# Context stage of a token mixer and expert kernel: four row buffers, earlier statistics, two banks for the first products, scatter one step earlier, first token loads of the next stage behind their own rows

## The chip, the core and the metric

The kernel runs on one core of a Trainium2 chip. TensorE (PE in the profile) multiplies, VectorE (DVE), ScalarE (ACT) and GpSimd (POOL) work on elements, SyncE (SP) only issues transfers; GpSimd issues the indirect ones. They run side by side and wait for one another on semaphores. The metric is the device time of one execution, in microseconds (us).

## What is computed

2048 tokens of width 512 go through two blocks. The first, which the change touches, is this (cut from the reference):

```python
x = x + _L0_xattn_ref(_layernorm(x), token_ids, ctx, ctx, ctx)

def _L0_xattn_ref(hidden_states, token_ids, Wg, Wu, Wd):      # Wg = Wu = Wd = ctx, 4 matrices of 512 x 512
    expert_ids = jnp.minimum(jnp.clip(token_ids, 0, 24999) // 6250, 3)
    for e in range(4):
        g = jax.nn.silu(jnp.einsum('bsd,fd->bsf', hidden_states, Wg[e]))
        u = jnp.einsum('bsd,fd->bsf', hidden_states, Wu[e])
        y = jnp.einsum('bsf,df->bsd', g * u, Wd[e])
        out = jnp.where((expert_ids == e)[..., None], y, out)
```

The second block normalizes x again, adds a shared gated product and the four best of 32 experts for every token, and a residual.

## The kernel before, in words

**Stages.** `context` is the first block of instructions, `shared_routing_and_experts` the second. All five engines meet at a barrier between the two; none starts the second before each has come to the end of its list in the first.

**The context stage.** First the tokens are sorted by group: counts and ranks by small products on TensorE and some thirty small operations on VectorE, which end in a list of row numbers (`gather1`, `scatter1`; semaphore `listed` at 1) and a table with the group of every tile and the number of tile pairs (`listed` at 2). A tile is 128 tokens of one group. The inputs make 18 tiles, n = 0 to 17. Matrices are split into a high and a low half, so that a product is three matmuls: 12 for one 128x512 result over 512 inputs (lines 222 to 224). `high(e)` on ScalarE and `low(e)` on VectorE (line 550) split the four context matrices; `low(2)` and `low(3)` run inside the first steps.

For each tile: gather of 128 rows of x by GpSimd (L381); `stats1`, mean and variance, on VectorE (L630, L633); `rstd1`, inverse root, scale and bias, three instructions on GpSimd (L386 to L391); `keep`, a copy of the rows for the residual, and `h`, the normalized rows, on ScalarE (L512, L529); `t1`, four transposes ("the turn") on TensorE (L447), whose result ScalarE and VectorE split into halves (`t1hi`, `t1lo`); `g1`, 12 matmuls into `ps_z`; `silu` on ScalarE and `a`, its product with `ps_z`, on VectorE (L645); `t2`, the turn of a, with `t2hi` and `t2lo`; `g2`, 12 matmuls into `ps_y`; `x1`, the sum with the kept rows and its statistics, on VectorE (L659 to L665); `rstd2` on GpSimd (L398 to L405); `x2` and `base` on ScalarE (L534, L539), `hn` on VectorE (L671); `scatter`, the indirect write of 128 rows to `hb_dram` by GpSimd (L413), which takes its row numbers from a copy made by `rows` (L642).

**What sets the order.** `pipeline` (in the listing) writes each engine's list. In step k an engine does each of its parts, in the order of its list, for tile k minus the part's skew. The first 12 steps are written out, the others up to step 17 run in a loop, then the rest is written out. TensorE has `[("t1", 3), ("t2", 5), ("g1", 4), ("g2", 6)]`, ScalarE `[("base", 9), ("x2", 8), ("t1hi", 3), ("t2hi", 5), ("keep", 2), ("weights", 0), ("h", 2), ("silu", 4)]`. `weights` splits a piece of the shared weights in steps 6, 7 and 8 (ScalarE L507).

**Buffers.** Gathered rows have two buffers, so gather n waits until `keep` and `h` of tile n - 2 are done. There is one bank `ps_z` for the first products. `hb`, what is scattered, has two buffers, and `base`, `rows` and `hn` of tile n wait until scatter n - 2 has landed. A `keep_busy` of 24 small matmuls, which are not used, stands ahead of the turns of tiles 0 and 1 and at the end of the stage.

**The end of the stage.** GpSimd waits until every scatter has landed and raises `stored`. On this TensorE starts its last `keep_busy` and SyncE loads the first four tiles of the next stage, tokens 0 to 511, from `hb_dram` (L339). The next stage turns its 16 tiles, by token number, in pairs with the routing logits of the pair before; tiles 4 to 15 are loaded by SyncE (L781) when a turn has freed the buffer.

## Time and profile before

| | us |
|---|---|
| median of 3 runs (lowest to highest) | 703.03 (700.66 to 703.36) |
| profiled execution, its own time | 702.91 |
| its span, first to last instruction | 701.2 |
| TensorE busy, matmuls | 628.1 (90%) |
| VectorE busy | 439.6 (63%) |
| ScalarE busy | 368.2 (53%) |
| GpSimd busy | 333.8 (48%) |
| mean granted TensorE clock, share of full | 0.975 |

The page of the profile cuts the span in 40 equal slices of 17.5 us. The context stage fills the first nine and a half of them. In its line of the granted clock all slices show 9 tenths or more but the tenth one, which shows 6, and the last. TensorE's busy time counts overlapping matmuls once and is no measure of how well it is used. The chain of waits follows the execution back from its last instruction; where it names an engine, that engine's work ended last there.

### The profile page before, as it was taken

The page shows a single profiled execution, that of the slowest core. Times are in us where ns is not written, and L with a number is a line of the kernel's source. Part 1 is how long each engine was busy: PE and PEld are TensorE (multiplying, and loading weights), DVE is VectorE, ACT ScalarE, POOL GpSimd, SP SyncE. Part 2 cuts the span into 40 slices and gives each one's busy share as a digit, 9 for nine tenths or more (in the row PEclk, how much of TensorE's full clock was granted, in tenths as well). Part 3 has the DMA queues.
Part 4 walks back from the last instruction along what each step waited for, and adds up shares of the span by engine and source line. Part 5 has one row for each costly group of instructions (what it writes and reads, how often), then busy time and mean ns, then how long its engine had stood idle before and what let it go on. Part 6 is the DMA issues. An engine that isn't in the chain of part 4 may idle for free.

```text
span 701.2 us, 15255 instructions
## 1 busy us (share of the span) xinstructions
PE 628.1 (90%) x3239; PEld 510.7 (73%) x3241; DVE 439.6 (63%) x1019; ACT 368.2 (53%) x637; POOL 333.8 (48%) x373
## 2 busy tenths in 40 slices
PE   2489999962999999799999999999999999999990
PEld 2368888852877887588878788788787688788870
DVE  7558787661799998365565565675465565655620
ACT  4357766533533322356665655765565565656530
POOL 2537777652002111545646456546546546465632
PEclk9999999996999999999999999999999999999995
DMA  6511332324793653667799788997777997988645
GB/s 243 181 46 41 118 106 90 116 110 141 241 344 49 147 136 46 137 180 208 203 240 266 207 266 205 278 279 202 211 205 184 277 269 195 269 218 219 108 62 70
DMA packets 35790, 124.69 MB, mean 178 GB/s; under 512 B 4784, under 2 KB 5936, under 8 KB 31152
## 3 DMA queue, kind: packets, MB, share of 16 engines
q0 software_dynamic: 24256, 59.26, 38.8%
q1 hardware_dynamic: 11504, 65.09, 26.4%
q8 instruction: 12, 0.20, 0.1%
q14 instruction: 18, 0.15, 0.1%
HBM read 90.51 MB, written 39.06 MB: 185 GB/s over the span
## 4 chain that ended last, share of the span: by engine, by line
PE 50%; DMA 20%; issue 10%; DVE 8%; POOL 6%; POOLq 2%; ACT 2%; DVEq 1%; ACTq 0%; SPq 0%
PE sps_gu L222 8%; PE sps_gu L224 7%; PE sps_gu L223 7%; DMA out<-r_oh,e_sidx 6%; DMA out<-r_rank,e_sidx 5%; DMA out<-normw,e_sidx 4%; PE sps_t L222 3%; PE sps_t L224 3%; PE sps_t L223 3%; PE sps_rank L866 2%; PE ps_z L222 2%; PE ps_z L224 2%; PE ps_z L223 2%; DMA raw<-in_experts_w 1%; PE sps_table L866 1%
## 5 line engine op out<-in xcount | busy, mean ns | idle before, releaser
L1275 DVE TENSOR_TENSOR wl<-raw,wh x87 | 105.7, 1225 | 58.6 <-ACT wh L1062 54.2
L222 PE MATMUL sps_gu<-wh,s_xth 128*128 x320 | 132.4, 414 | 2.5 <-DVE s_xtl L1258 2.1
L224 PE MATMUL sps_gu<-wh,s_xtl 128*128 x320 | 126.1, 394 | 0.0
L223 PE MATMUL sps_gu<-wl,s_xth 128*128 x320 | 125.0, 391 | 0.0
L854 POOL DMA_INDIRECT out<-r_oh,e_sidx x40 | 68.0, 1701 | 97.3 <-issue 64.1
L1062 ACT ACTIVATE wh<-raw x87 | 91.1, 1060 | 18.2 <-DMA raw<-in_experts_w 9.4
L840 POOL DMA_INDIRECT both<-hb_dram,e_gidx x76 | 84.1, 1106 | 31.7 <-issue 17.4
L222 PEld LDWEIGHTS sps_gu<-wh,s_xth 128*128 128x128 f32 x320 | 60.2, 188 | 14.5 <-issue 4.5
L1037 ACT ACTIVATE both<-sps_gu 128x256 f32<-128x256 f32 x80 | 30.7, 384 | 76.0 <-PE sps_gu L224 76.0
L222 PE MATMUL sps_t<-wh,s_ath 128*128 x160 | 69.6, 435 | 0.5
L224 PEld LDWEIGHTS sps_gu<-wh,s_xtl 128*128 128x128 f32 x320 | 60.1, 188 | 13.7
L223 PEld LDWEIGHTS sps_gu<-wl,s_xth 128*128 128x128 f32 x320 | 60.4, 189 | 10.5
L818 POOL DMA_DIRECT2D out<-both x16 | 14.1, 884 | 103.1 <-ACT both L1025 52.9
L224 PE MATMUL sps_t<-wh,s_atl 128*128 x160 | 63.1, 394 | 0.0
L223 PE MATMUL sps_t<-wl,s_ath 128*128 x160 | 62.7, 392 | 0.0
L1255 DVE TENSOR_TENSOR both<-both,sps_gu 128x256 f32<-128x256 f32 x80 | 33.3, 416 | 44.4 <-ACT both L1037 43.9
L1258 DVE TENSOR_TENSOR s_xtl<-sps_rank,s_xth 128x512 fp32r<-128x512 f32 x40 | 27.4, 686 | 37.9 <-ACT s_xth L1041 37.9
L854 POOL DMA_INDIRECT out<-normw,e_sidx x20 | 34.9, 1744 | 31.8 <-DMA out<-r_oh,e_sidx 28.1
L1049 ACT ACTIVATE r_oh<-sps_t,weight 128x512 f32<-128x512 f32 x40 | 27.4, 686 | 29.1 <-PE sps_t L224 19.6
L854 POOL DMA_INDIRECT out<-r_rank,e_sidx x20 | 31.6, 1581 | 22.8 <-DVE e_gidx L1248 9.5
L224 PEld LDWEIGHTS sps_t<-wh,s_atl 128*128 128x128 f32 x160 | 30.0, 188 | 6.8
L1258 DVE TENSOR_TENSOR s_xtl<-sps_cols,s_xth 128x512 fp32r<-128x512 f32 x40 | 27.5, 688 | 11.8 <-ACT s_xth L1041 11.6
(305 smaller groups left out, 1428.1 us busy)
## 6 DMA issues: line engine op xcount, KB each, us to landing
raw<-in_experts_w SPq DMA_DIRECT2D x32, 1536.0 KB, 8.1
craw<-in_ctx_w SPq DMA_DIRECT2D x4, 1024.0 KB, 8.2
both<-hb_dram SPq DMA_DIRECT2D x16, 256.0 KB, 3.6
out<-hb_dram SPq DMA_DIRECT2D x4, 1024.0 KB, 17.8
out<-both POOLq DMA_DIRECT2D x16, 256.0 KB, 4.2
both<-hb_dram,e_gidx POOLq DMA_INDIRECT x76, 5.8
out<-r_oh,e_sidx POOLq DMA_INDIRECT x40, 5.4
sraw<-in_sg SPq DMA_DIRECT2D x1, 512.0 KB, 5.4
```

The lines of the kernel that those rows point to most:

```text
L222: pe.matmul(acc, left_hi, right_hi, start=start, stop=False)
L223: pe.matmul(acc, left_hi, right_lo, start=False, stop=False)
L224: return pe.matmul(acc, left_lo, right_hi, start=False, stop=stop)
L840: pool.indirect_dma_start(e_xg[:, t.ring], None, hn_rows, bass.IndirectOffsetOnAxis(ap=gidx[:, t.ring:t.ring + 1], axis=0)).then_inc(e_gx[ ...
L854: pool.indirect_dma_start(m.out, bass.IndirectOffsetOnAxis(ap=sidx[:, t.ring:t.ring + 1], axis=0), e_y[t.ring], None, compute_op=ALU.add). ...
L866: mm = pe.transpose(dst[:, c * P:(c + 1) * P], src[:, c * P:(c + 1) * P], m.ident[:])
L1037: nc.scalar.activation(a[:, t.par], ps_gu[t.par][:, 0:INNER], ACT.Silu).then_inc(e["sil"], 1)
L1049: nc.scalar.activation(e_y[t.ring], e_py[t.par][:], ACT.Copy, scale=m.weight2[:, bass.ds(t.n, 1)]).then_inc(e["y"], 1)
L1062: nc.scalar.activation(m.wh[:, bass.ds(x % W_SETS, 1), ROWS[part], :], m.raw[:, bass.ds(x % 2, 1), ROWS[part], :], ACT.Copy).then_inc(e["h ...
L1255: dve.tensor_tensor(a[:, t.par], a[:, t.par], ps_gu[t.par][:, INNER:D], ALU.mult).then_inc(e["a"], 1)
L1258: dve.tensor_tensor(e_xtl[:, t.par].rearrange("p c n -> p (c n)"), e_t1[t.par][:], e_xth[:, t.par].rearrange("p c n -> p (c n)").bitcast(F ...
L1275: dve.tensor_tensor(m.wl[:, w, ROWS[part], :], m.raw[:, bass.ds(x % 2, 1), ROWS[part], :], m.wh[:, w, ROWS[part], :].bitcast(F32), ALU.sub ...
```

## The change

It touches the context stage and the first waits of SyncE in the next one.

- Gathered rows have four buffers for tiles 0 to 3 (`slot`, `landed`); from tile 4 on the first two alternate as before. `hb` moves into the space of the last raw context matrix (`craw`), `x2` gets a place of its own.
- GpSimd gathers tile 0, then 1 and 2 together, then 3 behind the first inverse root (`in_front`). VectorE does the statistics of tile 2 right behind those of tile 1. ScalarE does h of tile 1 right behind h of tile 0, ahead of the high half of tile 0.
- `ps_z` has two banks; `g1` of a tile no longer waits for `a` of the tile before, and TensorE's order is t1, g1, t2, g2.
- VectorE's order is `rows`, `hn`, `stats1`, ..., and `third` (which holds `low(2)`) stands behind the low halves. `scatter` has skew 9 instead of 10 and stands between `rstd1` and `rstd2`.
- A small reduction (`spread`) over the ranks, a product on TensorE and three operations on VectorE give the number of the last tile that holds a token of the first 512. SyncE's first four loads wait for as many scatters, and for statistics, kept copy and h of all tiles, and no longer for `stored`. The wait for all scatters stands in the next stage, ahead of the load of tile 4.
- TensorE's last `keep_busy` waits for the last x2.

The diff, cut to its core; the renamed semaphores and tensors are left out:

```diff
+        craw = sb("craw", [P, E1, C, D])
+        xg = m.tokens
...
-        x2 = m.tokens[:, 2:4]
-        hb = sb("c_hb", [P, 2, 2, D])
+        x2 = sb("c_x2", [P, 2, D])
+        hb = craw[:, E1 - 1].rearrange("p c n -> p (c n)").rearrange("p (s a n) -> p s a n", s=2, a=2)
...
-        ps_t1, ps_t2, ps_z = (ps(n, [P, D]) for n in ("ps_t1", "ps_t2", "ps_z"))
+        sidx = m.sidx1
+        ps_t1, ps_t2 = (ps(n, [P, D]) for n in ("ps_t1", "ps_t2"))
+        ps_z = [ps(f"ps_z{i}", [P, D]) for i in range(2)]
...
+        def slot(t):
+
+            return t.n if isinstance(t.n, int) and t.n < RING else t.par
+
+        def landed(eng, t):
+
+            eng.wait_ge(gx[slot(t)], 16 if isinstance(t.n, int) and t.n < RING else 16 * t.half)
+
+        def in_front(n):
+
+            if not isinstance(n, int) or n > RING - 1:
+                return ()
+            return {0: (0,), 1: (1, 2), 2: (3,), 3: ()}[n]
...
-            for q in gx:
+            for q in gx[0:2]:
...
-            sp.wait_ge(m.s["stored"], 1)
+            sp.wait_ge(m.s["early"], 1)
+            tiles = number_of_pairs(sp, m.tab1[0:1, 1, 0:1], MAX1) * 2
+            reach_of_first = sp.value_load(m.tab1[0:1, 1, 1:2], min_val=2, max_val=MAX1)
+            sp.wait_ge(s["stat1"], tiles)
+            sp.wait_ge(s["xr"], tiles)
+            sp.wait_ge(s["h"], tiles)
+            m.carry(sp)
+            sp.wait_ge(hbs[0], 16 * ((reach_of_first + 1) // 2))
+            sp.wait_ge(hbs[1], 16 * (reach_of_first // 2))
             for i in range(RING):
                 sp.dma_start(m.tokens[:, i], m.hb_dram[i * P:(i + 1) * P, 0:D]).then_inc(m.s[f"rows{i}"], 16)
...
-                if part == "gather":
-                    wait(pool, s["xr"], t.n - 1)
-                    wait(pool, s["h"], t.n - 1)
-                    wait(pool, gx[t.par], 16 * t.half)
+                if part == "gather" and isinstance(t.n, int) and t.n < RING:
+                    pool.wait_ge(m.s["listed"], 1)
+                    for n in in_front(t.n):
+                        pool.indirect_dma_start(xg[:, n], None, m.x, bass.IndirectOffsetOnAxis(ap=m.gather1[:, n:n + 1], axis=0)
+                                                ).then_inc(gx[n], 16)
+                elif part == "gather":
+                    left = t.n - RING if isinstance(t.n, int) and t.n < RING + 2 else t.n - 2
+                    pool.wait_ge(s["xr"], left + 1)
+                    pool.wait_ge(s["h"], left + 1)
+                    pool.wait_ge(gx[t.par], 16 * (t.half - 1))
                     if moving(t.n):
                         pool.wait_ge(s["gi"], t.n - STATIC + 1)
                         rows = gidx[:, t.par:t.par + 1]
                     else:
-                        wait(pool, m.s["listed"], 1)
                         rows = m.gather1[:, t.n:t.n + 1]
                     m.carry(pool)
...
-            pipeline(pool, pairs, [("scatter", 10), ("rstd1", 2), ("rstd2", 7), ("gather", 0)], emit)
-            m.carry(pool)
-            count = number_of_pairs(pool, m.tab1[0:1, 1, 0:1], MAX1)
-            for q in hbs:
-                pool.wait_ge(q, 16 * count)
-            pool.sem_inc(m.s["stored"], 1)
+            pipeline(pool, pairs, [("rstd1", 2), ("scatter", 9), ("rstd2", 7), ("gather", 0)], emit)
...
+            pe.wait_ge(m.s["spread"], 1)
+            pe.matmul(ps_spread, spread[:, 0:1], m.ident[:], start=True, stop=True).then_inc(m.s["spread_row"], 1)
...
-                        keep_busy(pe, m, ps_z, WARM)
+                        keep_busy(pe, m, ps_z[1], WARM)
...
-                    wait(pe, s["a"], t.n)
-                    product(ps_z, hth, htl, t).then_inc(s["g1"], 1)
+                    wait(pe, s["a"], t.n - 1)
+                    product(ps_z[t.par], hth, htl, t).then_inc(s["g1"], 1)
...
-            pipeline(pe, pairs, [("t1", 3), ("t2", 5), ("g1", 4), ("g2", 6)], emit,
+            pipeline(pe, pairs, [("t1", 3), ("g1", 4), ("t2", 5), ("g2", 6)], emit,
...
-            pe.wait_ge(m.s["stored"], 1)
-            keep_busy(pe, m, ps_z, WARM)
+            pe.wait_ge(s["x2"], 2 * number_of_pairs(pe, m.tab1[0:1, 1, 0:1], MAX1))
+            keep_busy(pe, m, ps_z[0], WARM)
...
-                    act.wait_ge(gx[t.par], 16 * (t.half + 1))
+                    if isinstance(t.n, int) and 1 <= t.n < LED:
+                        return
+                    landed(act, t)
...
+                elif part == "h" and isinstance(t.n, int) and t.n < LED:
+                    for n in range(LED) if t.n == 0 else ():
+                        if n >= 1:
+                            act.wait_ge(gx[n], 16)
+                            nc.scalar.activation(xr[:, n], xg[:, n], ACT.Copy).then_inc(s["xr"], 1)
+                        act.wait_ge(s["bias1"], n + 1)
+                        act.wait_ge(gx[n], 16)
+                        nc.scalar.activation(h[:, n], xg[:, n], ACT.Identity, bias=rs1[:, n, 2:3], scale=rs1[:, n, 1:2]).then_inc(s["h"], 1)
...
+            dve.tensor_reduce(spread[:, 0:1], sel[:, 1, 0:RING], AX.X, ALU.max).then_inc(m.s["spread"], 1)
...
+            dve.wait_ge(m.s["spread_row"], 1)
+            k(dve.tensor_reduce(spread[0:1, 1:2], ps_spread, AX.X, ALU.max))
+            k(dve.tensor_scalar(spread[0:1, 2:3], spread[0:1, 1:2], 1.0, 2.0, ALU.add, ALU.max))
+            dve.tensor_copy(m.tab1[:, 1, 1:2], spread[0:1, 2:3]).then_inc(m.s["early"], 1)
...
+                    if isinstance(t.n, int) and t.n < RING:
+                        for n in in_front(t.n):
+                            dve.wait_ge(gx[n], 16)
+                            wait(dve, s["bias1"], n - 1)
+                            dve.bn_stats(stat[:, 0, n % 2, :], xg[:, n]).then_inc(s["stat1"], 1)
+                            dve.wait_ge(s["stat1"], n + 1)
+                            dve.bn_aggr(mv[:, 0, n % 2, :], stat[:, 0, n % 2, :]).then_inc(s["mv1"], 1)
+                        return
+                    landed(dve, t)
...
-            pipeline(dve, pairs, [("stats1", 2), ("index", 0), ("third", 0), ("x1", 7), ("t1lo", 3), ("t2lo", 5), ("rows", 9), ("hn", 9), ("weights", 0), ("a", 4)], emit)
+            pipeline(dve, pairs, [("rows", 9), ("hn", 9), ("stats1", 2), ("index", 0), ("x1", 7), ("t1lo", 3), ("t2lo", 5), ("third", 0), ("weights", 0), ("a", 4)], emit)
...
+            pairs = number_of_pairs(sp, m.tab1[0:1, 1, 0:1], MAX1)
+            for q in ("stored0", "stored1"):
+                sp.wait_ge(m.s[q], 16 * pairs)
```

On GpSimd, the head of the stage, before and after: L381 and L400 are gathers, L386 to L391 and L418 to L423 the first inverse root of a tile.

```order
L381 DMA both<-in_x,gather 128x512 [waits chain0,listed]
L381 DMA both<-in_x,gather 128x512 [waits listed]
L386 TENSOR_SCALAR c_rs<-c_mv 128x1 [waits c_mv1]
L388 TENSOR_TENSOR c_rs<-c_rs,minus_half 128x1 [waits c_var1]
L391 TENSOR_SCALAR c_rs<-c_mv,c_rs 128x1 [waits c_rstd1]
L381 DMA both<-in_x,gather 128x512 [waits listed,c_gx0,c_xr,c_h]
```

```order
L400 DMA both<-in_x,gather 128x512 [waits chain0,listed]
L400 DMA both<-in_x,gather 128x512 [waits listed]
L400 DMA both<-in_x,gather 128x512
L418 TENSOR_SCALAR c_rs<-c_mv 128x1 [waits c_mv1]
L420 TENSOR_TENSOR c_rs<-c_rs,minus_half 128x1 [waits c_var1]
L423 TENSOR_SCALAR c_rs<-c_mv,c_rs 128x1 [waits c_rstd1]
L400 DMA both<-in_x,gather 128x512 [waits listed]
```

The third gather moved ahead of the first inverse root, and the third and fourth no longer wait for h (`c_h`) or the kept copy (`c_xr`).

On VectorE, the same place: `ctl` is a low half of a context matrix, `c_halves` the low half of a turned tile, `tab` the table whose entry the register load reads.

```order
L550 TENSOR_TENSOR ctl<-craw,cth 128x2048 [waits ctx_hi]
L189 TENSOR_LOAD tab [waits listed]
L189 ISA x2
L630 BN_STATS c_stat<-both 128x6 [waits c_gx0]
L633 BN_AGGR c_mv<-c_stat 128x2 [waits c_stat1]
L630 BN_STATS c_stat<-both 128x6 [waits c_gx1]
L633 BN_AGGR c_mv<-c_stat 128x2 [waits c_stat1]
L550 TENSOR_TENSOR ctl<-craw,cth 128x2048 [waits ctx_hi]
L648 TENSOR_TENSOR c_halves<-ps_t,c_halves 128x512 [waits c_t1hi]
```

```order
L589 TENSOR_TENSOR ctl<-craw,cth 128x2048 [waits ctx_hi]
L654 TENSOR_REDUCE spread<-ps_prefix 1x1 [waits spread_row]
L655 TENSOR_SCALAR spread<-spread 1x1 [waits chain1]
L656 CAST tab<-spread 1x1 [waits chain1]
L190 TENSOR_LOAD tab [waits listed]
L190 ISA x2
L677 BN_STATS c_stat<-both 128x6 [waits c_gx0]
L679 BN_AGGR c_mv<-c_stat 128x2 [waits c_stat1]
L677 BN_STATS c_stat<-both 128x6 [waits c_gx1]
L679 BN_AGGR c_mv<-c_stat 128x2 [waits c_stat1]
L677 BN_STATS c_stat<-both 128x6 [waits c_bias1,c_gx2]
L679 BN_AGGR c_mv<-c_stat 128x2 [waits c_stat1]
```

Three operations stand between `low(1)` and the register load, and the statistics of tile 2 have taken the place of `low(2)`, which now follows the low half of tile 0.

On GpSimd, the end of the stage, before and after: L413 and L445 are scatters, the others the second inverse root of a tile (L398 to L405, L430 to L437).

```order
L404 TENSOR_SCALAR c_affine<-c_rs 128x1 [waits c_rstd2]
L405 TENSOR_SCALAR c_affine<-c_rs,c_mv 128x2
L413 DMA hb_dram<-c_hb,c_sidx 2048x1024 [waits c_base,c_hn,c_hb1,c_si]
L89 ISA
L413 DMA hb_dram<-c_hb,c_sidx 2048x1024 [waits c_base,c_hn,c_hb0,c_si]
L413 DMA hb_dram<-c_hb,c_sidx 2048x1024 [waits c_base,c_hn,c_hb1,c_si]
L189 TENSOR_LOAD tab
L189 ISA x2
L421 ISA
L259 UNCONDITIONAL_BRANCH [waits c_hb0,c_hb1]
```

```order
L445 DMA hb_dram<-craw,sidx 2048x1024 [waits c_base,c_hn,stored1,c_si]
L430 TENSOR_SCALAR c_rs<-c_mv 128x1 [waits c_mv2,c_x2]
L431 TENSOR_SCALAR c_rs<-c_mv 128x1
L433 TENSOR_TENSOR c_rs<-c_rs,minus_half 128x2 [waits c_var2]
L436 TENSOR_SCALAR c_affine<-c_rs 128x1 [waits c_rstd2]
L437 TENSOR_SCALAR c_affine<-c_rs,c_mv 128x2
L89 ISA
L445 DMA hb_dram<-craw,sidx 2048x1024 [waits c_base,c_hn,stored0,c_si]
L445 DMA hb_dram<-craw,sidx 2048x1024 [waits c_base,c_hn,stored1,c_si]
L260 UNCONDITIONAL_BRANCH
```

Three scatters stood behind the inverse root of the last tile, and behind them a wait for all landings; now two stand behind it, one has moved ahead of it, and GpSimd leaves the stage without that wait.

## Rows read from the trace of the kernel before

**Rows 1.** windows: length, busy PE PEld DVE ACT POOL (instructions), granted clock, DMA share, GB/s

```profile
32.00:45.00 13.00, 7.95 (x35) 5.86 (x34) 6.74 (x10) 4.99 (x9) 6.21 (x8) 0.87 0.24 61
...
152.00:172.00 20.00, 2.74 (x24) 2.47 (x24) 4.22 (x10) 3.96 (x5) 7.96 (x14) 0.57 0.35 138
```

**Rows 2.** chain that ended last: start, length, what; turns of two steps

```profile
50.38 0.87 PE ps_t L447 x8
...
56.75 0.87 PE ps_t L447 x8
```

**Rows 3.** timeline of the head: start, length, engine, line [idle before]; last: the chain

```profile
15.72 1.31 DVE L203 SCALAR_TENSOR_TENSOR tb1f<-tb1f 1x11 f32<-1x11 f32 x7
...
17.68 2.27 DVE L550 TENSOR_TENSOR ctl<-craw,cth 128x2048 fp32r<-128x2048 f32 x1
...
19.88 0.68 DVE L630 BATCH_NORM_STATS2 c_stat<-both 128x6 f32<-128x512 f32 x1
...
21.37 2.74 PE L230 MATMUL ps_z<-before_b,ones_b 128*128 128x128 bf16 x24 [7.91 <-DVE c_mv L633]
...
22.61 1.93 POOL L391 TENSOR_SCALAR c_rs<-c_mv,c_rs 128x1 f32<-128x1 f32 x1 [0.21 <-POOL c_rs L388]
...
29.96 0.49 PE L222 MATMUL ps_z<-cth,c_halves 128*128 x1
...
32.45 2.70 POOL L388 TENSOR_TENSOR c_rs<-c_rs,minus_half 128x1 f32<-128x1 f32 x1
...
36.52 0.66 PE L447 MATMUL ps_t<-ident,c_h 128*128 128x128 f32 x4 [3.54 <-ACT c_h L529]
...
39.34 0.43 PE ps_z L224
```

**Rows 4.** register load of the pair count (line 189), by operation

```profile
L189 DVEq TENSOR_LOAD <-tab x1: 553/553/553, 17.8 to 17.8; - x1
```

**Rows 5.** timeline of ACT in a step that also splits shared weights

```profile
57.72 0.59 ACT L524 ACTIVATE c_halves<-ps_t 128x512 fp32r<-128x512 f32 x1
...
58.72 1.06 ACT L507 ACTIVATE wh_s<-sraw 128x1024 fp32r<-128x1024 f32 x1
...
59.66 0.81 ACT L529 ACTIVATE c_h<-both,c_rs 128x512 f32<-128x512 f32 x1
```

**Rows 6.** timeline of POOL and ACT in the steps of the loop

```profile
98.21 1.22 POOL L401 TENSOR_TENSOR c_rs<-c_rs,minus_half 128x2 f32<-128x2 f32 x1
...
102.08 1.02 POOL L413 DMA_INDIRECT hb_dram<-c_hb,c_sidx  x1 [0.30 <-issue]
...
108.80 1.02 POOL L413 DMA_INDIRECT hb_dram<-c_hb,c_sidx  x1 [0.30 <-issue]
...
125.20 0.82 ACT L529 ACTIVATE c_h<-both,c_rs 128x512 f32<-128x512 f32 x1 [2.30 <-POOL c_rs L391]
```

**Rows 7.** end of the stage: chain pieces for the DMAs and x1, timeline for the rest

```profile
150.63 3.42 DMA hb_dram<-c_hb,c_sidx
...
151.25 0.39 PE L224 MATMUL ps_y<-cth,c_halves 128*128 x1
...
155.25 0.70 DVE c_x L659
...
159.81 0.81 ACT L534 ACTIVATE both<-c_x,c_affine,c_rs 128x512 f32<-128x512 f32 x1 [0.96 <-POOL c_affine L405]
...
165.52 3.21 DMA hb_dram<-c_hb,c_sidx
...
168.82 2.74 PE L230 MATMUL ps_z<-before_b,ones_b 128*128 128x128 bf16 x24 [17.18 <-POOLq L422]
...
168.84 1.76 SPq L339 DMA_DIRECT2D both<-hb_dram  x4
```

**Rows 8.** timeline of PE at the start of the next stage

```profile
172.13 1.33 PE L866 MATMUL sps_t<-ident,both 128*128 128x128 f32 x8 [0.57 <-PEq L259]
...
176.89 1.30 PE L866 MATMUL sps_t<-ident,both 128*128 128x128 f32 x8
```

30 lines of the change are left out of this document (15 added, 15 removed).

## Prediction, made before the changed kernel was run

> **What bounds the kernel now.** I read the slices of the page first: TensorE is busy nearly everywhere, and its clock is clearly below full in one slice only, the one in which the context stage ends. So I took windows of that stage [rows 1]. Between 32 and 45 us TensorE works 7.95 of 13 us, and between 152 and 172 us only 2.74 of 20, all of it the dummy products that warm it, at a granted clock of 0.57: mostly the lower, 1.2 GHz, of its two levels. Between the two it never rests: the chain of waits shows one tile a step, every 6.37 us [rows 2]. Of that the two turns take 0.87 and each group of twelve products (6.37 - 0.87) / 2 = 2.75. Nothing in the change touches this work, so the stage can only win at its head, at its end, and lose in the middle. I write E for the end of the last product of the stage, 151.25 + 0.39 = 151.64 us [rows 7].
>
> The head is a line of handovers [rows 3]: `low(1)` on VectorE until 19.95, statistics of tile 0, inverse root on GpSimd (one of its instructions takes 1.93 us beside `low(2)`), h, turn, first product at 29.96. Tile 2 is late because its rows were only asked for when tile 0 was normalized, and then its inverse root takes 2.70 us beside `low(3)`: TensorE waits 3.54 us until 36.52. The turn of tile 4, with which the even steps begin, comes at 50.38 [rows 2].
>
> At the end [rows 7] x1 of the last tile waits for scatter 13 to land (150.63 + 3.42), then GpSimd and ScalarE bring x2 at 159.81, the last scatter goes at 165.52 = E + 13.9 and lands 3.21 later, at E + 17.1. Only then do the warming products and the first token loads start, at 168.8. The next stage turns its first tile at 172.13 = E + 20.5 and its fifth at 176.89 = E + 25.3 [rows 8].
>
> **The head, step by step.** Four gathers without a wait for a free buffer take tiles 2 and 3 off the critical path, and `low(2)` now stands behind the first low half, not beside the first inverse root. Against that, VectorE has four more small operations ahead of the first statistics. Such operations stand 1.31 / 7 = 0.19 us apart [rows 3]: one ahead of `low(0)`, three behind `low(1)`, 0.75 in all. The register load of the pair count, today hidden under `low(1)`, now stands behind them, 0.55 us [rows 4] and some 0.25 for the two register steps behind it. Statistics of tile 0 move from 19.88 to about 21.4. The Trainium skill (DMA: Bandwidth & Descriptors, § Latency and other measured facts) gives about 0.6 us as the floor of such a load, near the trace's 0.55.
>
> From there, with durations of the same rows: mean and variance at 22.5, warming products until 25.3 (2.74), turn of tile 0 at 25.4. ScalarE now does h of tile 1 ahead of the high half of tile 0, so low half 0 is ready at 28.9, the first product starts at 29.4 (29.96 today) and ends at 32.3. The turn of tile 2 needs low half 1, which stands behind `low(2)` and the statistics of tile 3: 32.9. Twelve products follow at 33.4 at once (no a is needed with two banks), until 36.2; `low(3)` runs beside them. The turn of a(0) at 36.2, its high half, the kept copy and h of tile 3 on ScalarE in that order give the turn of tile 3 at 38.9; then 12 + turn + 12 products until 45.2, and behind the first piece of shared weights the turn of tile 4 at **45.7 instead of 50.38: 4.7 won**. The granted clock of 0.87 in this stretch today [rows 1] followed the 3.5 us of waiting; a product stood 0.43 apart then [rows 3] where 2.75 / 12 = 0.23 is the pace at 2.4 GHz. I count on full clock, since the longest gap in my line is 2.2 us. If seven products run at the lower level as now, 7 x 0.20 = 1.4 of the 4.7 are gone. At the other end, with the register load hidden, I would win 5.5.
>
> **The middle.** TensorE now turns a behind the first products instead of ahead of them. Within a step the order is t1, twelve products, t2, twelve products, so the high half of a starts at about +3.9 us, and the kept copy and h stand behind it on ScalarE: 1.0 for the first two, 0.8 for h [rows 5], h ready at +5.7, under the 6.37 of a step by 0.6. In the steps with a piece of shared weights 0.94 more lies between (58.72 to 59.66 [rows 5]), so the next turn is late by 0.35. One such step is in the 45.7 already, two follow: **0.7 lost**. Today h has over 2 us of room there and this cost nothing.
>
> GpSimd is the second thing in the middle. In the loop its scatters stand 6.72 apart [rows 6], more than TensorE's 6.37: it falls behind 0.35 each step, and by 125.20 h waits 2.30 us for it, just about when TensorE begins to lose (some 0.5 us in all before the end). The change keeps its instructions but gives it less room: `rows` and `hn` come first on VectorE and a comes later, so the statistics of a tile are ready some 2.7 us later in the step; in return h may come 0.6 later than today before TensorE waits. GpSimd's 6.7 us are 1.3 for the first inverse root, 1.4 for the scatter, 2.3 for the second root and 1.6 for the gather. The statistics are ready at +2.5 and the gather ahead of them ends at +2.8, so the first root is ready at +4.1; TensorE would wait from +5.5, a lead used up after four steps of the loop; from the fifth on each step costs 0.35, 0.9 in all, against today's 0.5: **0.4 lost**. Bounds: 0 if GpSimd's gaps shrink with the shorter issue, 3.2 if all nine steps with a scatter run at its pace.
>
> At this place one rule speaks against the change. In [rows 6] an instruction at 98.21 takes 1.22 us while VectorE does `hn` beside it. The Trainium skill (GPSIMD Engine Reference, § 8 Key points) says that GpSimd shares its SBUF interfaces with VectorE and contends with instructions of two SBUF inputs, as `hn` is. The trace agrees (2.70 beside `low(3)` too). By it a worse meeting of `hn` and GpSimd could add up to 0.5 us a step, 3 us in six steps of the loop; since `hn` runs once a step before and after, my sum has none.
>
> E then falls at 151.64 - 4.7 + 0.7 + 0.4 = 148.0.
>
> **The end, counted from E.** Scatter 13 goes ahead of the second inverse root instead of behind it and lands well before E, so x1 of tile 17 starts at +0.1, not at 155.25 = +3.6. It gains less than that behind it, because GpSimd has inverse root 16 until +2.0 and scatter 15 (1.1 us) ahead of inverse root 17: that ends at +5.8, x2 at +5.9 to +6.7 (today 159.81 = +8.2). The last scatter, behind hn and base of tile 17, goes at +7.5 instead of +13.9 and lands at **+10.8 instead of +17.1**.
>
> The warming products wait for x2, not for the last landing: +6.7. From their start to the first turn it takes 172.13 - 168.82 = 3.3 [rows 7, 8], so the next stage begins at +10.0 instead of +20.5. Its first four tiles are there: the loads wait for the last h (some 20 us ahead of E) and for the scatters that hold rows 0 to 511. The inputs give 108, 119, 131 and 1690 tokens to the four groups, 18 tiles, and the first 512 tokens end in the eighth, so this wait ends last at h. What is late next are tiles 4 on, since SyncE now waits for all scatters there: issue at +10.9, 3.3 until the first such load landed (168.84 to 172.13): +14.2. Four turns and the first logits end there too (+10.0 plus 4.0), so the fifth turn comes at about +14.5 instead of +25.3: **10.8 won**, or 9.5 if the twelve loads that now go out at once land one by one, 1.3 apart. From there the stage is TensorE's own work as before, and all later stages move with it. The new SyncE waits have nothing queued behind them but these loads.
>
> **Sum.** 4.7 - 0.7 - 0.4 + 10.3 (between 9.5 and 10.8) = 13.9 us. The profiled execution took 702.9 us, the median of the three is 703.0; 702.9 - 13.9 = **689.0**. Bounds of the terms: head 3.3 to 5.5, middle -3.9 to -0.2, end 9 to 11: 8.4 to 16.3 won, or 686.6 to 694.5.
>
> **Rivals.** (a) *GpSimd sets the pace of the whole middle*, from the first scatter, and meets `hn` worse: 3.2 + 3 lost there instead of 0.4, and the head's clock falls: 689.0 + 5.8 + 1.4 = 696.2. For it speaks the 6.72 us; against it that GpSimd had over 2 us in hand until 125 us. (b) *The early loads do not help*: the next stage waits for transfers in any case, as its first turns do today. Then the fifth turn comes as far behind the last landing as today, 25.3 - 17.1 = 8.2, at 10.8 + 8.2 = +19, and 4.5 of the gain are lost: 693.5. Against it speaks that SyncE's queue is empty from 24 us on. (c) *Slower*: the clock. The new order puts short gaps into every step (h ready only 0.6 ahead), where today there are none from 45 to 150 us, with full clock. If such gaps bring the clock down, a product costs 0.43 instead of 0.23 us, 24 of them 4.8 us a step: three such steps eat the 13.9, and five make 689.0 + 24 = 713. Both low stretches of this stage followed a gap of over 3 us, so I give it little. The Trainium skill has such a case (TensorE: Matmul & The Clock Gate, § A second HAM failure mode: psum-queue depth-cycling): a kernel that went round its PSUM banks and paused briefly between groups swung between the two clock levels. No row here shows it. (d) *More*: the register load is hidden, GpSimd keeps up, and routing starts ahead of a busy stretch of DMA: 685.
>
> **How the numbers follow.** The forecast's case 0.62, (a) with its milder forms 0.14, (b) 0.08, (c) 0.04, (d) 0.07, and 0.05 that gains and losses cancel within 3.5 us. About 0.5% (3.5 us) is what a measurement of this kernel can tell from no change. Faster by more than that: 0.62 + 0.14 + 0.08 + 0.07 = 0.91, less 0.03 for later stages that I did not follow: 0.88; same 0.05 + 0.02 = 0.07; slower 0.04 + 0.01 = 0.05. The range 685 to 697 leaves out (c), the cancelling case and the ends of (a) and (d).
>
> **What would show it.** The turn of tile 4 at 45 to 46 us (above 48: the head is wrong); no clock below 1 between 30 and 45; steps of 6.4 us with one or two of 6.7 to 6.8 where shared weights are split, and again in the last two or three steps of h; E near 148; x2 of the last tile 6 to 7 us behind E, the last scatter 7 to 8 behind; SyncE's four loads issued near 125 to 130; the first turn of the next stage 10 us behind E and the fifth near 14.5. Steps of 6.7 all along would be (a), a late fifth turn (b), a granted clock below 1 in the middle (c).

## The result and the profile after

The changed kernel takes **696.72 us** (median of 4 runs, 695.64 to 696.88) where the kernel before took 702.58 beside it: ratio 0.9926, 95% interval 0.9906 to 0.9947. Run again beside the experiments it was 697.26 against 701.71, 0.9941 (0.9911 to 0.9970). So it is faster by 4 to 6 us. I had forecast 689.0, 13.9 less: the sign and the range hold, the size is more than twice what came. The profiled execution after took 696.7 us, its span 694.8 us (before: 701.2). Three executions beside the experiments, of 712 to 1286 us, were in a slower state and are left out of the ratios.

These instants divide the difference. In this table and below, E is again the end of the last product of the stage, and "turn n" the turn of tile n. Turns are read from timelines: turn 4 of before is there at 50.22, where the chain of [rows 2] has the same one at 50.38.

| | before | forecast | after |
|---|---|---|---|
| turn of tile 4 of the context stage | 50.2 | 45.7 | 47.3 |
| E | 151.6 | 148.0 | 156.0 |
| last scatter issued | E + 13.9 | E + 7.5 | E + 8.3 |
| first turn of the next stage | E + 20.5 | E + 10.0 | E + 12.6 |
| fifth turn of the next stage | E + 25.3 = 176.9 | E + 14.5 = 162.5 | E + 18.0 = 174.0 |
| from the fifth turn to the end of the span | 524.3 | as before | 520.8 |

2.9 us were won in the head, **7.2 lost in the middle** (turn 4 to E: 108.6 us, before 101.4), 7.2 won at the end. That makes 2.9 at the fifth turn, not 14.4. Another 3.5 us of the two spans' difference arose in the last 520 us, whose code is unchanged but for SyncE's wait ahead of the load of tile 4.

Windows of the kernel after (length, busy PE, PEld, DVE, ACT, POOL, granted clock, DMA share, GB/s), which answer [rows 1]:

```profile
32.00:45.00 13.00, 10.63 (x48) 8.28 (x46) 7.19 (x11) 4.61 (x9) 5.48 (x8) 0.87 0.15 40
152.00:172.00 20.00, 10.11 (x59) 8.75 (x57) 8.12 (x17) 7.72 (x11) 9.29 (x19) 0.69 0.32 127
```

TensorE works 2.7 us more of the first window, as hoped, and yet its clock is 0.87, as before. The second window now holds real products until 156: the stage has slid into it.

Timeline of TensorE after, at turn 3 and at three turns of the loop (start, length, engine, line, operation [idle before <- what ended it]); compare [rows 3] and [rows 2]:

```profile
39.02 0.66 PE L476 MATMUL ps_t<-ident,c_h 128*128 128x128 f32 x4 [1.91 <-ACT c_h L568]
...
40.26 0.63 PE L223 MATMUL ps_z<-cth,c_halves 128*128 x1
40.69 0.63 PE L224 MATMUL ps_z<-ctl,c_halves 128*128 x1
...
87.26 0.66 PE L476 MATMUL ps_t<-ident,c_h 128*128 128x128 f32 x4 [0.41 <-ACT c_h L568]
...
94.50 0.65 PE L476 MATMUL ps_t<-ident,c_h 128*128 128x128 f32 x4 [0.63 <-ACT c_h L568]
...
101.80 0.66 PE L476 MATMUL ps_t<-ident,c_h 128*128 128x128 f32 x4 [0.54 <-ACT c_h L568]
```

After a gap of 1.91 us the products stand 0.43 us apart: that is the lower of the clock's two levels. In the loop a step takes 7.24 and 7.30 us instead of 6.37, and each turn waits for h. Why h is late shows GpSimd in the same stretch, which answers [rows 6]:

```profile
94.31 1.08 POOL L445 DMA_INDIRECT hb_dram<-craw,sidx  x1 [0.79 <-issue]
95.47 0.18 POOL L430 TENSOR_SCALAR c_rs<-c_mv 128x1 f32<-128x1 f32 x1
...
95.99 1.16 POOL L433 TENSOR_TENSOR c_rs<-c_rs,minus_half 128x2 f32<-128x2 f32 x1
...
98.34 1.09 POOL L413 DMA_INDIRECT both<-in_x,c_gidx  x1 [0.51 <-issue]
99.50 0.18 POOL L418 TENSOR_SCALAR c_rs<-c_mv 128x1 f32<-128x1 f32 x1
...
101.65 1.08 POOL L445 DMA_INDIRECT hb_dram<-craw,sidx  x1 [0.83 <-issue]
```

Here GpSimd waits for nothing that the profile shows ("issue"; I read it as the register work ahead of an indirect DMA, which the profile doesn't show by itself): it is never free, and its scatters (L445) stand 7.34 us apart. The idle time ahead of a scatter is 0.79 and 0.83, where [rows 6] had 0.30. The steps of TensorE were 6.4 us from turn 6 to turn 9, at 80.25, and 7.0 to 7.4 from there to turn 16; the loop starts at turn 9 (step 12). For ScalarE it reads like this, x2 waiting for the second inverse root and h for the first (waits between 60 and 150 us: total, times, longest):

```profile
ACT c_x L573 <- POOL c_affine L437: 22.7, 12, 2.4
...
ACT c_h L568 <- POOL c_rs L423: 5.2, 8, 0.7
```

The end of the stage, answering [rows 7 and 8]: GpSimd's last scatter, the end of each engine's list (L260, by operation: count, duration in ns, start), and TensorE's next turns.

```profile
164.21 0.97 POOL L445 DMA_INDIRECT hb_dram<-craw,sidx  x1 [0.88 <-DVE craw L723]
```

```profile
L260 ACTq DRAIN  x1: 1119/1119/1119, 162.1 to 162.1; - x1
L260 DVEq DRAIN  x1: 730/730/730, 162.6 to 162.6; - x1
L260 PEldq DRAIN  x1: 2125/2125/2125, 163.2 to 163.2; - x1
L260 POOLq DRAIN  x1: 4324/4324/4324, 164.0 to 164.0; - x1
```

```profile
162.58 2.74 PE L231 MATMUL ps_z<-before_b,ones_b 128*128 128x128 bf16 x24 [6.62 <-ACT c_x L573]
168.59 1.94 PE L921 MATMUL sps_t<-ident,both 128*128 128x128 f32 x8 [3.27 <-PEq L260]
```

TensorE was done at 165.3, but the barrier opened at 168.5 only: GpSimd's drain takes from 164.0 to 168.3. SyncE's four early loads had gone out at 137.9, so they were there; the next ones went out at 169.77, behind the barrier and the first turn.

The 3.27 us of idle time ahead of the first turn cost more than themselves. Windows of TensorE, before first, then after (length, busy, granted clock, DMA share, GB/s):

```profile
172.00:176.00 4.00, 3.14 (x21) 1.00 0.76 231
```

```profile
168.00:172.00 4.00, 3.41 (x17) 0.50 0.23 80
```

Before, the first turns ran at full clock; now they run at the lower level, and from the first to the fifth turn it takes 5.4 us instead of 4.8.

### The profile page after: what moved, and what is told of

It is laid out like the page before. It is cut to its first block, busy times and chain, and to the rows that moved or that the text cites. A ratio compares the mean times of both kernels' runs of the same rounds, so it can differ in the third digit from the quotient of the medians.

```text
span 694.8 us, 15275 instructions
## 1 busy us (share of the span) xinstructions
PE 632.7 (91%) x3242; PEld 512.0 (74%) x3243; DVE 442.1 (64%) x1023; ACT 366.8 (53%) x637; POOL 334.1 (48%) x373
## 4 chain that ended last, share of the span: by engine, by line
PE 41%; DMA 14%; issue 8%; DVE 4%; POOLq 2%; ACT 2%; POOL 1%; DVEq 1%; ACTq 1%
PE sps_gu L223 8%; PE sps_gu L225 8%; PE sps_gu L224 8%; DMA out<-r_oh,e_sidx 5%; DMA out<-normw,e_sidx 4%; PE sps_t L223 3%; PE sps_t L225 3%; PE sps_t L224 3%; DMA out<-r_rank,e_sidx 2%; PE sps_rank L921 2%; PE sps_table L921 1%; DMA both<-hb_dram,e_gidx 1%; PE sps_cols L921 1%; PE sps_table L976 1%; ACT wh L1117 1%
## 5 line engine op out<-in xcount | busy, mean ns | idle before, releaser
L895 POOL DMA_INDIRECT both<-hb_dram,e_gidx x76 | 82.4, 1085 | 31.4 <-issue 17.4
L225 PEld LDWEIGHTS sps_gu<-wh,s_xtl 128*128 128x128 f32 x320 | 60.0, 188 | 13.9
L873 POOL DMA_DIRECT2D out<-both x16 | 14.2, 885 | 101.2 <-ACT both L1080 58.0
L1310 DVE TENSOR_TENSOR both<-both,sps_gu 128x256 f32<-128x256 f32 x80 | 33.4, 417 | 44.6 <-ACT both L1092 40.8
L909 POOL DMA_INDIRECT out<-r_rank,e_sidx x20 | 31.7, 1585 | 25.4 <-DMA out<-normw,e_sidx 13.5
L1104 ACT ACTIVATE r_oh<-sps_t,weight 128x512 f32<-128x512 f32 x40 | 27.4, 686 | 29.8 <-PE sps_t L225 18.4
## 6 DMA issues: line engine op xcount, KB each, us to landing
out<-hb_dram SPq DMA_DIRECT2D x4, 1024.0 KB, 17.4
```

What stands on the lines that cost most here:

```text
L225: return pe.matmul(acc, left_lo, right_hi, start=False, stop=stop)
L895: pool.indirect_dma_start(e_xg[:, t.ring], None, hn_rows, bass.IndirectOffsetOnAxis(ap=gidx[:, t.ring:t.ring + 1], axis=0)).then_inc(e_gx[ ...
L909: pool.indirect_dma_start(m.out, bass.IndirectOffsetOnAxis(ap=sidx[:, t.ring:t.ring + 1], axis=0), e_y[t.ring], None, compute_op=ALU.add). ...
L1104: nc.scalar.activation(e_y[t.ring], e_py[t.par][:], ACT.Copy, scale=m.weight2[:, bass.ds(t.n, 1)]).then_inc(e["y"], 1)
L1310: dve.tensor_tensor(a[:, t.par], a[:, t.par], ps_gu[t.par][:, INNER:D], ALU.mult).then_inc(e["a"], 1)
```

## The experiments

"E" and the turns are from each one's own trace; the ratio is to the kernel before on the same chip.

| run | median us | ratio (95%) | turn 4 | E | last scatter | fifth turn |
|---|---|---|---|---|---|---|
| before | 701.7 to 702.0 | 1 | 50.2 | 151.6 | E + 13.9 | 176.9 |
| after, again | 697.26 | 0.9941 (0.9911, 0.9970) | 47.3 | 155.9 | E + 8.3 | 174.1 |
| GpSimd's old order | 698.43 | 0.9973 (0.9949, 0.9997) | 47.1 | 150.3 | E + 13.2 | 173.0 |
| TensorE's old order | 695.61 | 0.9927 (0.9902, 0.9952) | 48.4 | 153.6 | E + 8.3 | 171.0 |
| VectorE's old order | 709.76 | 1.0124 (1.0085, 1.0162) | 45.6 | 161.9 | E + 13.0 | 184.0 |
| all three old orders | 698.64 | 0.9953 (0.9925, 0.9981) | 48.2 | 149.4 | E + 13.9 | 173.3 |
| mix, VectorE old | 701.00 | 0.9990 (0.9967, 1.0013) | 48.4 | 153.4 | E + 12.9 | 176.6 |
| mix, VectorE new | 692.77 | 0.9867 (0.9840, 0.9894) | 48.2 | 149.1 | E + 8.3 | 167.3 |
| last scatter behind the barrier | 698.84 | 0.9961 (0.9939, 0.9982) | 47.0 | 155.7 | E + 12.2 | 173.7 |
| mix, VectorE old, last scatter behind | 700.80 | 0.9978 (0.9956, 1.0000) | 48.3 | 153.4 | E + 16.8 | 175.8 |
| mix, VectorE new, gap filled | 688.89 | 0.9824 (0.9781, 0.9866) | 46.6 | 147.4 | E + 8.3 | 165.8 |
| the same, end filled too | 688.79 | 0.9814 (0.9775, 0.9853) | 46.9 | 147.8 | E + 8.3 | 165.1 |
| before, late order only | 695.09 | 0.9891 (0.9850, 0.9933) | 49.9 | 151.1 | E + 8.5 | 171.7 |

### Which of the three orders costs the middle?

**GpSimd.** The edit, alone on the kernel after:

```
-pipeline(pool, pairs, [("rstd1", 2), ("scatter", 9), ("rstd2", 7), ("gather", 0)], emit)
+pipeline(pool, pairs, [("scatter", 10), ("rstd1", 2), ("rstd2", 7), ("gather", 0)], emit)
```

> The kernel after, with GpSimd's order of before: the scatter right behind the gather again (one step later in the pipeline). In the kernel after GpSimd works without rest in the loop, 7.3 us a step, and 0.8 us stand idle ahead of each scatter where before it was 0.30. Theory G (GpSimd's own length of a step sets the middle, and half a microsecond of it is the scatter's register work that the gather used to hide): turns of h in the loop 6.8 apart instead of 7.3, E some 4 us earlier (about 151.5), the whole about 693. Theory T (TensorE's new order makes h late through ScalarE; GpSimd only follows): steps stay at 7.2 to 7.3, E within 1 us of 155.5, and the last scatter goes later behind E as in the kernel before, so the whole is no faster or up to 3 us slower.

Measured: steps of 6.4 to 6.7 in the loop, E at 150.3, 5.6 us earlier. GpSimd in the loop of this kernel:

```profile
107.48 1.34 POOL L413 DMA_INDIRECT both<-in_x,c_gidx  x1 [0.62 <-issue]
109.13 1.02 POOL L445 DMA_INDIRECT hb_dram<-craw,sidx  x1 [0.30 <-DVE c_mv L685]
...
112.14 0.71 POOL L433 TENSOR_TENSOR c_rs<-c_rs,minus_half 128x2 f32<-128x2 f32 x1
...
115.59 1.02 POOL L445 DMA_INDIRECT hb_dram<-craw,sidx  x1 [0.31 <-DVE c_mv L685]
```

The scatters stand 6.46 to 6.66 apart. Two things differ from the rows of after: the idle time ahead of the scatter is 0.30 instead of 0.8, now that a gather of 1.1 to 1.3 us stands ahead of it, and not an operation of 0.27 us; and the second inverse root (L433) takes 0.71 instead of 1.16, since it no longer runs beside `hn`. The gather is up to 0.25 longer. 0.5 + 0.45 less this is the 0.7 to 0.9 by which a step is shorter. Theory G holds for the middle. Its 693 for the whole does not: the last scatter goes one step later again, E + 13.2, as I had foreseen under theory T alone, and the end gives back what the middle won. 698.43 is no better than the kernel after.

**TensorE.** `[("t1", 3), ("g1", 4), ("t2", 5), ("g2", 6)]` back to `[("t1", 3), ("t2", 5), ("g1", 4), ("g2", 6)]`:

> The kernel after, with TensorE's order of before: the turn of a ahead of the first products of the step. Theory T (its new order makes h late): the steps of the loop fall from 7.3 to 6.4 to 6.7, E 5 to 6 us earlier, about 150, the whole about 691. Theory G (GpSimd's length of a step): the loop stays at 7.2 to 7.3; only the first steps lose their 0.4 us of waiting for h, and E is 0.5 to 2 us earlier, the whole 695 to 696.

Measured: steps of 6.33 to 6.36 as far as turn 12 at 99.2, where the kernel after waited 0.4 to 0.5 us in the steps with shared weights and lost from turn 9 on; then 6.9 and 7.2 to 7.3 here too, as theory G says. E is 2.4 us earlier although turn 4 is 1.1 later. So both are right for a part: TensorE's new order takes away the lead that ScalarE needs (3.5 us between turn 4 and E), GpSimd's new order makes the step too long (5.4). Undone together they give 7.5 to 7.8, as the next runs show.

**VectorE.** `rows` and `hn` back behind the low halves:

> The kernel after, with rows and hn on VectorE behind the low halves again, as before, so that the statistics of a tile come early in the step. Theory G: GpSimd's own work is the same, so the loop stays at 7.2 to 7.3; its lead is longer by the 2.7 us by which the statistics come earlier, and E is 1 to 2.7 us earlier; the second inverse root meets hn elsewhere, 0.5 us a step either way. Theory S (late statistics are what holds GpSimd up each step): steps of 6.7, E 4 to 5 us earlier, about 151, the whole about 692.

Both expectations failed, and this is the worst of all: E at 161.9, 6 us later, and from turn 7 on steps of 6.9 to 8.0 us, most of them 7.35. Timeline of one step:

```profile
95.62 1.08 POOL L445 DMA_INDIRECT hb_dram<-craw,sidx  x1 [1.43 <-DVE craw L723]
...
98.80 0.81 ACT L573 ACTIVATE c_x<-c_x,c_affine,c_rs 128x512 f32<-128x512 f32 x1 [2.58 <-POOL c_affine L437]
99.52 0.58 ACT L551 ACTIVATE c_halves<-ps_t 128x512 fp32r<-128x512 f32 x1
100.00 0.59 ACT L555 ACTIVATE c_halves<-ps_t 128x512 fp32r<-128x512 f32 x1
100.13 0.69 DVE L700 TENSOR_TENSOR c_halves<-ps_t,c_halves 128x512 fp32r<-128x512 f32 x1 [0.71 <-ACT c_halves L551]
...
101.40 0.68 DVE L723 TENSOR_TENSOR craw<-c_x,normw 128x512 f32<-128x512 f32 x1
...
103.00 1.08 POOL L445 DMA_INDIRECT hb_dram<-craw,sidx  x1 [0.79 <-issue]
```

It is a closed ring. Ahead of the second inverse root GpSimd now has the scatter, which needs `hn` (L723); behind the inverse root wait x2 and, on ScalarE, both high halves (L551, L555); behind these the low halves on VectorE; and behind them, in the old order, `hn`. A turn round the ring is 7.35 us, whatever TensorE does. Each scatter of this trace up to 160.44 is issued 0.9 to 1.0 us behind the end of its `hn`; in the loop of the kernel after it is 5.1 to 5.4 us. In the loop GpSimd's own list is just as long as the ring, and E is late mostly by what follows it: from turn 16 to E it takes 29.3 us, in the kernel after 24.9. `hn` in front on VectorE is what opens it: that part of the change belongs to the new place of the scatter.

This trace also settles the head. Turn 3 waits 1.90 us as in the kernel after, the work is the same, and turn 4 comes at 45.59, where I had put it (45.7). Windows of TensorE, after first, then this kernel (length, busy, granted clock, DMA share, GB/s):

```profile
37.00:40.00 3.00, 1.09 (x9) 1.00 0.34 87
40.00:43.00 3.00, 3.00 (x9) 0.52 0.00 0
```

```profile
37.00:40.00 3.00, 1.14 (x7) 1.00 0.33 87
40.00:43.00 3.00, 3.00 (x16) 1.00 0.00 0
```

The same gap was followed by the lower clock in four of the five traces with TensorE's new order and not in this one, so the 1.7 us between the two depend on more than the gap's length. In the five traces with TensorE's old order and nothing put into the gap, it was 2.08 us long, and the lower clock followed in every one.

**All three.**

> The kernel after with all three orders of before (GpSimd, TensorE, VectorE); four row buffers, early statistics, two banks for the first product and the early loads stay. If the middle's loss lies in the orders alone: from the turn of tile 4 to E 101.3 to 102 us as before instead of 108.2, E about 149 and the whole near 690, unless the end gives some back (the scatter of the last tile comes a step later on GpSimd: last scatter at E + 12 instead of E + 8.7, then 693). If the two banks or the buffers hurt, E stays above 152.

Measured: 101.2 us from turn 4 to E. The middle's loss lies in the orders alone; four buffers and two banks cost nothing there. The end goes as the expectation's doubt says, and worse (E + 13.9, fifth turn E + 23.9): 698.64. Against [rows 8] with its E + 25.3, the early loads bring 1.3 us there.

### Can the middle of before be had with the end of after?

The mix keeps TensorE's old order, and GpSimd's has two forms: in the loop the scatter stands behind the gather, in the steps written out behind the loop it stands ahead of the second inverse root.

```
+pipeline(pool, pairs, [("rstd1", 2), ("rstd2", 7), ("gather", 0), ("scatter", 9)], emit,
+         tail=[("rstd1", 2), ("scatter", 9), ("rstd2", 7)])
```

First with VectorE's old order, then with its new one:

> The kernel after, with the orders of before on TensorE, VectorE and in GpSimd's loop, but with the new order (scatter ahead of the second inverse root) in the steps behind GpSimd's loop. If the middle and the end are separate terms, as the sum of the prediction takes them: turn of tile 4 at 48.2, E at 149.4 and steps of 6.35 as with all orders of before; from E on as in the kernel after: last scatter E + 8.3, fifth turn E + 18, which is 167.4; the whole 9.5 us under before, about 692.5 where before runs 702, and about 5 under the kernel after. Rival: what is won here is given back by the later stages, as 1 to 3 us were in the runs with the old orders; then 695 to 696.

> The same as the mix of orders, but VectorE keeps its new order (rows and hn first). Theory G says that VectorE's order does not change GpSimd's work: steps of 6.4 until late, GpSimd's scatters 6.7 to 6.8 apart, E within 1.5 us of 149.4. If late statistics or the meeting of hn with the second inverse root cost, as rival (a) of the prediction says, GpSimd's steps are longer than 6.9 and E is 151 to 153.

With the old order the expectation failed, 701.0: the steps are 6.35 until turn 16, and then the ring closes. Timeline of the second step behind GpSimd's loop:

```profile
129.60 0.68 DVE L723 TENSOR_TENSOR craw<-c_x,normw 128x512 f32<-128x512 f32 x1
...
131.15 1.08 POOL L445 DMA_INDIRECT hb_dram<-craw,sidx  x1 [2.77 <-DVE craw L723]
...
134.25 0.82 ACT L573 ACTIVATE c_x<-c_x,c_affine,c_rs 128x512 f32<-128x512 f32 x1 [3.05 <-POOL c_affine L437]
```

The scatters from 123.92 to 151.95 stand 7.2, 7.3, 6.7 and 6.7 us apart, E comes at 153.4. With the new order there is no ring: E at 149.1, last scatter E + 8.3, fifth turn at 167.3, the **692.77** that I had expected of the other one. It is faster than the kernel after, by 4 to 5 us, and the terms do add up once the ring is open. Late statistics cost nothing here; GpSimd's scatters in the loop stand 6.4 to 7.1 apart.

### What holds the barrier?

The scatter of tile 17 becomes the first instruction of GpSimd's next block:

```
+                    if t.off == -1:
+                        m.last_scatter = (sidx[:, t.par:t.par + 1], hb[:, t.par].rearrange("p a n -> p (a n)"), hbs[t.par])
+                        return
...
         def _(pool):
+            rows, src, sem = m.last_scatter
+            pool.indirect_dma_start(m.hb_dram, bass.IndirectOffsetOnAxis(ap=rows, axis=0), src, None,
+                                    bounds_check=TOKENS - 1, oob_is_err=False).then_inc(sem, 16)
             pool.wait_ge(s["base"], 16 * RING)
```

> The kernel after, with the scatter of tile 17 issued as the first instruction of GpSimd's next block, behind the barrier, instead of as the last of this one. Theory D (the barrier opens late because GpSimd's drain waits for its scatters to land: 4.3 us in the kernel after): the drain ends when the scatter of tile 16 has landed, and the first turn of the next stage comes 2.5 to 3.5 us earlier, at about E + 10, with no idle time behind the warming products; the fifth turn gains little, 0 to 1 us, since its load still waits for the last scatter, which now goes out at about E + 10. The whole within 1 us of the kernel after. Rival: the drain is a fixed cost of the block's end (4 us whatever is in flight); then the first turn stays at E + 12.6 and the fifth comes 2 to 3 us later.

```profile
L260 POOLq DRAIN  x1: 5164/5164/5164, 161.7 to 161.7; - x1
```

```profile
167.17 1.94 PE L927 MATMUL sps_t<-ident,both 128*128 128x128 f32 x8 [2.13 <-PEq L260]
```

The drain's row begins while the scatter of tile 16 (161.96 to 163.04) is still being issued and ends at 166.9. The barrier opens 1.4 us earlier than after (1.1 counted from E), not 2.5 to 3.5, and 2.1 us of idle time remain. In the kernel before every scatter had landed when the drain began, and it took 3.0 us all the same (3.0 also in the kernel with the late order by itself, below):

```profile
L259 POOLq DRAIN  x1: 3012/3012/3012, 168.8 to 168.8; - x1
```

From the end of the last scatter's issue to the end of the drain it is 3.1 us after (165.2 to 168.3) and 3.8 here (163.0 to 166.9). So theory D fell: the drain is not simply the wait for the last landing. The rival is nearer: the drain ends 3.0 to 3.9 us behind GpSimd's last work in all fourteen traces. What the 0.7 to 0.8 more is where the last scatter was moved (3.9 in the next run), stays open. The fifth turn did as expected, 173.7, since its load now waits for the moved scatter. The same edit on the mix with VectorE's old order:

> The mix of orders together with the last scatter behind the barrier. If the three effects add up: E at 149.4, first turn at E + 10, fifth turn at E + 17 to E + 18, the whole within 1.5 us of the mix alone, about 692; if the drain costs more than the load of tile 4 waits for the scatter, up to 2 us better, 690.

It had to fail with that mix: the ring is there, E at 153.4, 700.8. The barrier opens 1.2 us earlier than without the edit, the fifth turn comes 0.8 earlier.

### The gap in the head, and the end

> The changed kernel itself, unedited, so that it stands beside the others on one chip: 6 us under before (0.9926 of it, as measured), E at 156, the fifth turn at 174. In its first trace the stages behind the fifth turn took 3.5 us less than in the trace of before; if that is chance of the transfers in the experts' loop, this trace shows another value, 0 to 3.5 us.

The second trace of the kernel after is the first one's twin up to the fifth turn (174.1), the gap and the low clock of the head included; from there to its end it takes 522.0 us, 1.2 more.

```
                 elif part == "t2":
+                    if isinstance(t.n, int) and t.n == 0:
+                        keep_busy(pe, m, ps_y[1], 16)
                     pe.wait_ge(s["a"], t.n + 1)
```

> The mix of orders with VectorE's new order, and 16 dummy products (1.8 us) ahead of the turn of a of tile 0, where TensorE stood idle 2.1 us until 35.78 and the granted clock then fell to its lower level for 9 products. If the fall of the clock is the cost: no clock below 1 between 30 and 49 us, turn of tile 4 at 46.4 to 46.6 instead of 48.2, E at 147.3, the whole 1.7 us under the mix (0.984 of before). Rival: the dummies hold up the turn of a, or what follows waits for tile 3 in any case: turn of tile 4 within 0.4 of 48.2.

Windows of the mix first, then of the mix with the gap filled:

```profile
34.00:37.00 3.00, 1.22 (x8) 0.99 0.02 8
37.00:40.00 3.00, 3.00 (x9) 0.50 0.34 87
```

```profile
34.00:37.00 3.00, 1.81 (x19) 1.00 0.03 12
37.00:40.00 3.00, 2.63 (x14) 1.00 0.31 87
```

The 16 products took 1.06 us, not 1.8, and left 1.19 idle, and that was enough: full clock, turn 4 at 46.6, E at 147.4: both 1.6 us earlier than in the mix, as expected. The median is **688.89**, 3.9 us under the mix's on another chip, 3.0 by the two ratios; 1.5 of these are there at the fifth turn, the others lie behind it, and the two ratios' intervals overlap, so I count on 1.6 only. It beats both kernels.

> As the one with the gap filled, and 42 instead of 24 dummy products at the end of the stage, so that TensorE is busy until just ahead of the barrier's opening (E + 7 to E + 11.9). If the low clock there costs: the first four turns of the next stage take 0.66 each instead of up to 1.06, the fifth turn comes 0.4 to 1 us earlier, the whole 0.5 to 1 us under the one without. Rival: the fifth turn waits for its load, nothing is gained; or the added products delay the barrier, up to 1 us later.

Here 42 dummy products run at the end: the first turns of the next stage take 0.6 instead of 1.06 and the fifth comes at E + 17.4 instead of E + 18.4. Window of TensorE, to be compared with the 0.50 of the kernel after:

```profile
160.00:164.00 4.00, 2.21 (x19) 1.00 0.40 128
```

TensorE's gap ahead of the first turn is 1.77 us here instead of 3.26, and the clock is full. The whole is 688.79: the 1 us is not to be seen in it.

### The late order by itself

> The kernel before, with only these parts of the change: rows and hn first on VectorE, and, in the steps behind GpSimd's loop, the scatter a step sooner and ahead of the second inverse root. No early loads, two row buffers, one bank. If the end is gained by this order: E stays at 151.6, the last scatter goes at E + 8.3 instead of E + 13.9, the first turn comes at E + 15 and the fifth at E + 19.7 instead of E + 25.3, the whole 5.5 us under before, 0.992. If the early loads are what brings the end, the whole is within 2 us of before.

```profile
159.53 0.96 POOL L413 DMA_INDIRECT hb_dram<-c_hb,c_sidx  x1 [0.88 <-DVE c_hb L671]
```

```profile
165.86 1.97 PE L866 MATMUL sps_t<-ident,both 128*128 128x128 f32 x8 [0.66 <-DMA both<-hb_dram]
...
171.69 1.04 PE L866 MATMUL sps_t<-ident,both 128*128 128x128 f32 x8
```

E + 8.5, E + 14.8 and E + 20.6: as expected but for 0.9 at the fifth turn. The whole is 695.09, no slower than the full change (697.26 on the same chip). Two changes of order, the scatter a step sooner behind the loop and `hn` first on VectorE, are worth as much as all of it, as far as the intervals tell. Measured against the gap-filled mix (fifth turn E + 18.4), the early loads and the rest of the change's end add 2.3 us.

## Why the prediction was wrong in size

**The head: right, but for the clock.** Turn 0 at 25.3 (forecast 25.4), turn 2 at 33.2 (32.9), turn 3 at 39.0 (38.9), each within 0.35 us. The step that failed is "I count on full clock, since the longest gap in my line is 2.2 us": the gap came as forecast, 1.91 us, nine products ran at the lower level behind it, and that took 1.6 us, for which the 1.4 in my own sentence was nearly the price. My rows had only gaps of over 3 us; that a shorter one leaves the clock alone, nothing in them showed. In the run with VectorE's old order, where the clock didn't fall, turn 4 came at 45.59 for my 45.7.

**The middle: one term mis-sized, 0.4 for 6.** The term for h on ScalarE was sound: I put turns 0.35 late in the steps with shared weights and found 6.79 and 6.90 instead of 6.37, then 6.40 to 6.44. About 1.1 instead of 0.7. The term for GpSimd failed in the sentence "The change keeps its instructions but gives it less room". It kept the instructions, but not what each costs. From [rows 6] I had 6.72 us a step, with 0.30 of idle time ahead of the scatter. That 0.30 held only because a gather stood ahead of it. Moved behind a 0.27 us operation the scatter waits 0.8. The trace of before had a sign of it, which I passed over: from 127.60 to 154.58, behind its last gather, its scatters follow an operation of 0.26 us and wait 0.5 to 0.6:

```profile
127.60 1.08 POOL L413 DMA_INDIRECT hb_dram<-c_hb,c_sidx  x1 [0.52 <-issue]
```

Seven steps from 80.25 to 131.07 took 50.8 us instead of 7 x 6.37 = 44.6: **6.2 lost**. I had carried the instruction to its new place with the gap of its old one. Against my 6.72 the longer step is 3.8 of the 6.2. The other 2.4 are the lead of GpSimd, which I had lasting four steps of the loop: turn 10, the first in the loop, was late already. With TensorE's old order it lasted until turn 12.

This is rival (a), GpSimd as the pace of the whole middle with the clock's fall in the head. I had priced it at 6.2 for the middle and 1.4 for the clock, 696.2 in all, and given it 0.14. That its price for the middle came out is in part chance: it was made of nine steps at 6.72 (3.2) and a worse meeting with `hn` (3), and what cost the time was the 0.5 ahead of the scatter and the lost lead. Beside `hn` the second inverse root takes 1.16 instead of 0.71. The Trainium skill's rule on this (GPSIMD Engine Reference, § 8 Key points: contention with VectorE instructions of two SBUF inputs) is borne out by that pair of rows, 0.45 us a step near the 0.5 which I had allowed it and then left out of the sum because "`hn` runs once a step before and after". But the meeting exists before too: from 98 us on one GpSimd instruction of each step is 0.3 to 0.5 longer there (1.22 for 0.71 in [rows 6]), as in the loop of the kernel after. So against before it is no loss; the 0.5 ahead of the scatter is.

**The end: 3.5 too little.** x2 came at E + 5.8 and the last scatter at E + 8.3 (forecast 5.9 to 6.7 and 7.5). The step that failed is the 3.3 us "from their start to the first turn", and it is 2.6 of the 3.5. I read them in [rows 7, 8] as the warming products' own time. But GpSimd's drain of 3.0 us ran beside them in the kernel before, both from 168.8 on. Now the warming products end at E + 9.4 and the drain, which counts from the last scatter's issue, at E + 12.4: first turn E + 12.6. From the first to the fifth turn I had 4.5 us and it took 5.4, since TensorE, idle 3.27 us before, worked at the lower clock; filled to a gap of 1.77 it took 4.7 at full clock. The load of tile 4 waits for the barrier and the first turn, not for the landing, and goes out at 169.77 = E + 13.8 instead of E + 10.9; still the fifth turn, at E + 18.0, follows the logits without idle time. Rival (b) gave nearly this place (+19) for another reason, that the early loads don't help, which is not what happened: the four tiles were there.

**The rest of the program.** I let it go by as unchanged. In fourteen traces the time from the fifth turn to the end of the span lies between 519.1 and 524.3, the latter being the kernel before. Two traces of one kernel (after) are 1.2 apart. Of the measured 5.9 us, 2.9 are there at the fifth turn, and up to 3.5 come from this stretch. What decides it was not tried; that the transfers of the experts' loop do is only a guess.

**The rivals.** (c), the clock of the middle, did not come: 1.00 from 46 us to E. Nor did (d): the first turn, and with it the register load, lay where I had put them. With the two orders and the gap mended the parts of the change do give 688.9 us. That it is the forecast's number is partly chance: E is where I had put it (147.4 for 148.0), the fifth turn 3.3 us later than forecast, and the stretch behind it shorter.

## What to carry to other kernels

When an instruction moves on GpSimd, price the idle time ahead of it anew: what its new neighbour is long enough to hide counts, not the gap of the old place; an engine whose step is only 5% longer than the bottleneck's has no room for half a microsecond. Before moving a step ahead of another one, follow the ring of engines that it closes, and look whether some engine's order has to move with it. At a barrier read the last row of every engine, drains too: it opens with the latest of them, not with the one on which your chain of waits ran.
